# A fused attention and mixture-of-experts layer on one Trainium2 core: the softmax division goes from VectorE to ScalarE, over four buffers, with a pair's two transposes in one step

## What is computed

```
scores = einsum('bhqd,bhkd->bhqk', qh, kh) * DH ** (-0.5)
window_mask = (j <= i) & (j >= i - W)          # W = 64
scores = where(window_mask, scores, -1e+30)
probs = softmax(scores, axis=-1)
out = einsum('bhqk,bhkd->bhqd', probs, vh)
...
x = x + tanh(g_xattn) * (out @ wo.T)
x = x + tanh(g_ffn) * moe(layernorm(x))
```

## Time and profile before

| what | value |
|---|---|
| median of 3 runs | 578.61 us (577.44 to 578.98) |
| the profiled execution | 576.19 us |
| its span, first to last instruction | 574.4 us |
| mean granted TensorE clock | 0.982 |
| attention, some 30 to 352 us: busy TensorE / VectorE / ScalarE / GpSimd | 284.4 / 273.1 / 188.2 / 187.2 us of 322 |

### The profile page before, as it was taken

The page is one execution under the profiler, slowest core; times in us unless marked ns, Lnnn a source line. Parts: engine busy times, 40 slices in busy tenths (PEclk is TensorE's granted clock), DMA queues, the critical chain, the costliest instruction groups (busy, mean ns, idle before and its releaser), DMA issues.

```text
span 574.4 us, 13053 instructions
## 1 busy us (share of the span) xinstructions
PE 526.0 (92%) x4914; PEld 458.3 (80%) x4914; DVE 416.1 (72%) x1139; ACT 292.8 (51%) x832; POOL 220.9 (38%) x123
## 2 busy tenths in 40 slices
PE   8968889999699999699897989989999999999997
PEld 5557677888597888588777878978998898899996
DVE  5987879779979879988968895655465646564444
ACT  3275556565375556366635775544445443533332
POOL 2897846447447545635834841620010001000000
PEclk9999989999999999899989989989999999999999
DMA  6621311111022011011201045600800090036000
GB/s 237 195 69 57 107 48 61 34 34 33 2 71 70 2 34 33 2 34 34 70 2 34 20 125 185 222 1 3 294 36 1 11 322 1 1 91 242 1 1 37
DMA packets 20173, 41.02 MB, mean 71 GB/s; under 512 B 2896, under 2 KB 3152, under 8 KB 20112
## 3 DMA queue, kind: packets, MB, share of 16 engines
q1 hardware_dynamic: 20112, 40.20, 22.4%
HBM read 30.62 MB, written 2.23 MB: 57 GB/s over the span
## 4 chain that ended last, share of the span: by engine, by line
PE 56%; DVE 24%; issue 11%; ACT 3%; POOL 3%; DMA 1%; SPq 0%; DVEq 0%; ACTq 0%; POOLq 0%
PE ring L761 37%; PE psS L761 8%; DVE arena L594 5%; DVE sneg L713 5%; DVE prob L725 4%; PE psO L959 3%; PE psS L928 3%; PE psT L940 3%; DVE xn L574 2%; DVE arena L591 2%; DVE wl L661 1%; DMA x<-in_x 1%; POOL wl L396 1%; POOL arena L415 1%; PE psT L901 1%
## 5 line engine op out<-in xcount | busy, mean ns | idle before, releaser
L498 ACT ACTIVATE prob<-sneg,nmax 128x128 f32<-128x128 f32 x256 | 99.8, 395 | 71.9 <-DVE nmax L713 70.7
L761 PE MATMUL ring<-xTh,wh 128*128 128x512 f32 x272 | 111.1, 408 | 4.9 <-POOL wl L396 2.3
L411 POOL TENSOR_TENSOR arena<-arena,sin 128x1024 f32<-128x1024 f32 (+1 forms) x34 | 78.0, 2295 | 93.0 <-DVE arena L591 93.0
L761 PE MATMUL ring<-xTl,wh 128*128 128x512 f32 x272 | 106.9, 393 | 0.0
L761 PE MATMUL ring<-xTh,wl 128*128 128x512 f32 x272 | 106.2, 390 | 0.0
L442 ACT ACTIVATE sneg<-ring 128x512 f32<-128x512 f32 x72 | 43.3, 601 | 109.5 <-PE ring L761 103.6
L640 DVE TENSOR_TENSOR prob<-sneg,arena 128x512 f32<-128x512 f32 x64 | 44.2, 690 | 69.1 <-ACT sneg L442 69.1
L415 POOL TENSOR_TENSOR arena<-arena 128x1024 f32<-128x1024 f32 (+1 forms) x34 | 85.4, 2513 | 2.7
L761 PE MATMUL ring<-wh,oTh 128*128 128x256 f32 x272 | 77.7, 286 | 1.4 <-DVE oTl L648 0.9
L725 DVE TENSOR_TENSOR prob<-prob,rinv 128x512 f32<-128x512 f32 x64 | 76.2, 1190 | 2.2
L761 PE MATMUL ring<-wl,oTh 128*128 128x256 f32 x272 | 76.0, 279 | 0.0
(11 more groups left out here) (111 smaller groups left out, 1123.9 us busy)
## 6 DMA issues: line engine op xcount, KB each, us to landing
arena<-gate_scratch SPq DMA_DIRECT2D x64, 256.0 KB, 6.3
raw<-in_e SPq DMA_DIRECT2D x18, 256.0 KB, 2.8
raw<-in_w SPq DMA_DIRECT2D x16, 256.0 KB, 2.9
arena<-arena SPq DMA_DIRECT2D x16, 256.0 KB, 3.1
arena<-arena SPq DMA_DIRECT2D x16, 192.0 KB, 3.4
craw<-in_ctx SPq DMA_DIRECT2D x4, 512.0 KB, 3.5
x<-in_x SPq DMA_DIRECT2D x4, 512.0 KB, 4.6
out<-x SPq DMA_DIRECT2D x8, 256.0 KB, 2.7
```

The source lines that it names most:

```text
L411: link(pool.tensor_tensor(part, part, sin[:, :].unsqueeze(1).to_broadcast(part.shape), ALU.mult))
L498: last = act.activation(prob[:, c % 3, t, :], sneg[:, c % 2, t, :], ACT.Exp, bias=nmax[:, c % 4, t:t + 1], scale=-1.0, accum_out=rsum[:, c ...
L761: last = pe.matmul(out, a, b, start=start and i == 0 and j == 0, stop=stop and i == n - 1 and j == 2, skip_group_check=check)
```

## The change

1. The multiplication of the probabilities goes from one VectorE instruction of 128x512 per head (L725) to four ScalarE instructions of 128x128, which are Copy with `rinv` as a scale per row. They stand in ScalarE's queue after the exponentials of the next head. VectorE keeps the reciprocal (`invert`).
2. `sneg`, `prob` and `rinv` have four buffers each. Two of `sneg` lie in `arena`.
3. VectorE does `score_max` for both heads of a pair in the even step.
4. The transposes of the pair `2p`, `2p+1` stand in step `2p + 3`: the first ahead of the jobs, the second after them, and likewise their copies out on ScalarE.
5. GpSimd's rotation of q stands at k = 1, that of k has its multiplication at k = 2 and its addition at k = 3.

The core of the diff:

```diff
-        prob = sb("prob", [P, 3, TT, P])
+        prob = sb("prob", [P, BUFS, TT, P])
...
+        transposed = {2 * p + 3: 2 * p for p in range(CHUNKS // 2)}
...
+            for c, jobs in steps:
+                u, k = divmod(c, G)
+                if u + 1 < UNITS:
+                    if k == 1:
+                        turn(0, u + 1)
+                        join(0, u + 1)
+                    if k == 2 and u:
+                        turn(1, u + 1)
+                    if k == 3 and u:
+                        join(1, u + 1)
+                for job in jobs:
+                    do(job)
...
+            def divide(c):
+                act.wait_ge(s_inv, c + 1)
+                for t in range(TT):
+                    last = act.activation(prob[:, c % BUFS, t, :], prob[:, c % BUFS, t, :], ACT.Copy,
+                                          scale=rinv[:, c % BUFS, t:t + 1])
+                last.then_inc(s_norm, 1)
...
             for c, jobs in steps:
-                if 2 <= c <= CHUNKS + 1:
-                    copy_transposed(c - 2)
+                if c in transposed:
+                    copy_transposed(transposed[c])
                 if c in attended:
                     round_att(attended[c])
                 if c < CHUNKS:
                     softmax_numerator(c)
+                if 1 <= c <= CHUNKS:
+                    divide(c - 1)
                 for job in jobs:
                     do(job)
+                if c in transposed:
+                    copy_transposed(transposed[c] + 1)
...
-                if c >= 2:
-                    dve.wait_ge(s_exp, c - 1)
+                if c >= BUFS:
+                    dve.wait_ge(s_exp, c - BUFS + 1)
...
-                dve.wait_ge(s_inv, c + 1)
-                dve.tensor_tensor(prob[:, c % 3, :, :], prob[:, c % 3, :, :],
-                                  rinv[:, c % 2, :].unsqueeze(2).to_broadcast([P, TT, P]),
-                                  ALU.mult).then_inc(s_norm, 1)
...
             for c, jobs in steps:
-                if c < CHUNKS:
+                if c < CHUNKS and c % 2 == 0:
                     score_max(c)
+                    score_max(c + 1)
                 if 1 <= c <= CHUNKS:
-                    divide(c - 1)
+                    invert(c - 1)
...
-                if 2 <= c <= CHUNKS + 1:
-                    transpose_probs(c - 2)
+                if c in transposed:
+                    transpose_probs(transposed[c])
                 for job in jobs:
                     do(job)
+                if c in transposed:
+                    transpose_probs(transposed[c] + 1)
```

More of the change, by code:

```diff
@@ L83, in build @@
         rw_parts = sb("rw_parts", [P, KC, 2, NR], F32R)
-        sizes = dict(swap=(2, 2, L), qT=(2, 2, L), kT=(2, 2, W + L), spare=(1, 2, 896),
+        sizes = dict(swap=(2, 2, L), qT=(2, 2, L), kT=(2, 2, W + L), idle=(1, 1, L), late=(2, TT, P), spare=(1, 1, 256),
                      v_al=(2, TT, GD), v_sh=(2, TT, GD))
@@ L91, in build @@
             at += a * b * c
-        idle = cuts["spare"][:, 0, 0, 0:L]
+        idle = cuts["idle"][:, 0, 0, :]
         swap = cuts["swap"]
@@ L96, in build @@
         gate_bc = arena[:, 0:NR * L].rearrange("p (e n) -> p e n", e=NR)
-        sneg = sb("sneg", [P, 2, TT, P])
-        prob = sb("prob", [P, 3, TT, P])
+        sneg_a = sb("sneg", [P, 2, TT, P])
+        sneg = [sneg_a[:, 0, :, :], sneg_a[:, 1, :, :], cuts["late"][:, 0, :, :], cuts["late"][:, 1, :, :]]
+        prob = sb("prob", [P, BUFS, TT, P])
         pT = sb("pT", [P, 4, TT, P])
@@ L390, in _, with turn, join @@
             pool.wait_ge(pool_init, 1)
+            def turn(i, n):
+                for done, pairs in rotations(n):
+                    part = swap[:, i, pairs, :]
+                    pool.wait_ge(qk_swap[i], done)
+                    link(pool.tensor_tensor(part, part,
+                                            sin[:, :].unsqueeze(1).to_broadcast(part.shape),
+                                            ALU.mult))
+            def join(i, n):
+                dst = (qT[:, n % 2, :, :], kT[:, n % 2, :, W:])[i]
+                for done, pairs in rotations(n):
+                    pool.wait_ge(qk_mul[i], done)
+                    pool.tensor_tensor(dst[:, pairs, :], dst[:, pairs, :], swap[:, i, pairs, :],
+                                       ALU.add).then_inc(qk_rot[i], 1)
             def do(job):
@@ L402, in do @@
                                        ALU.subtract).then_inc(c_lo, 1)
-                elif kind in "qk":
+                elif kind in "qk" and n < 1 + (kind == "k"):
                     i = "qk".index(kind)
-                    dst = qT[:, n % 2, :, :] if kind == "q" else kT[:, n % 2, :, W:]
                     if n == 0:
@@ L421, in do @@
                                        ALU.pow).then_inc(ln_rstd, 1)
-            for job in jobs_a + [j for n in range(NS, N + 2) for j in after[n]]:
+            for job in prologue:
                 do(job)
+            for c, jobs in steps:
[10 more added lines that the diff above has]
+                    do(job)
+            for n in range(NS, N + 2):
+                for job in after[n]:
+                    do(job)
         @block.scalar
@@ L494, in softmax_numerator @@
                 act.wait_ge(s_max, c + 1)
-                if c >= 3:
-                    act.wait_ge(p_pe, c - 2)
+                if c >= BUFS:
+                    act.wait_ge(p_pe, c - BUFS + 1)
                 for t in range(TT):
-                    last = act.activation(prob[:, c % 3, t, :], sneg[:, c % 2, t, :], ACT.Exp,
+                    last = act.activation(prob[:, c % BUFS, t, :], sneg[c % BUFS][:, t, :], ACT.Exp,
                                           bias=nmax[:, c % 4, t:t + 1], scale=-1.0,
@@ L709, in score_max @@
                     dve.wait_ge(in_const, consts)
-                if c >= 2:
-                    dve.wait_ge(s_exp, c - 1)
+                if c >= BUFS:
+                    dve.wait_ge(s_exp, c - BUFS + 1)
                 for t in range(TT):
-                    last = dve.tensor_tensor_reduce(sneg[:, c % 2, t, :], psS[c % 2][:, t, :],
+                    last = dve.tensor_tensor_reduce(sneg[c % BUFS][:, t, :], psS[c % 2][:, t, :],
                                                     mask[:, min(t, 1), :], -SCALE, -MASKED * 1e3,
@@ L939, in transpose_probs @@
                 for t in range(TT):
-                    last = pe.transpose(psT[:, t, :], prob[:, c % 3, t, :], ident[:, :])
+                    last = pe.transpose(psT[:, t, :], prob[:, c % BUFS, t, :], ident[:, :])
                 last.then_inc(p_pe, 1)
```

15 lines of the change are left out of this document (9 added, 6 removed).

## The result

The changed kernel takes **583.56 us** (median of 5, 581.28 to 585.40), the kernel before 577.58 (median of 5, 576.48 to 578.98): a ratio of **1.0099, with the 95% interval 1.0067 to 1.0131**. It is 6 us slower. The forecast was 589.0 with the range 572 to 604, and slower the likeliest sign.

A forecast was written before the change was run, and what follows sets the result against it. TensorE was taken as the bound, 31 us of its attention waits ending with VectorE. -2.1 (normal units) + 3.3 (norm units) + 6.4 (start) + 3.2 (end) = +10.8 on the profiled 576.2, so 587.0, median 589 us; range 572 to 604.

The forecast's parts named there:

- The bound, and the loop on ScalarE: Attention: TensorE bounds; its VectorE waits go, but `values` waits 0.8 us for the second head's copy behind ScalarE's division.
- rival 2: Attention: ScalarE, idle 42%, has room; half of the 31 us of waits go, none come; 563 us, chance 0.10.
- The copy's price: ScalarE's division: 0.30 us per 128x128 instruction, 1.2 us a head, 77 us in all.
- Rivals 1 and 4: ScalarE's division: cheap copies at 0.19 us, 575 us, chance 0.14; dear copies at 0.39 us, 607 us, chance 0.12.
- rival 1: ScalarE's division: cheap copies at 0.19 us an instruction, 0.44 us shorter a head; -14.5 us, 575 us, chance 0.14.
- Normal units: Seven units without a layer norm: 18.45 us each for 18.73, -0.3 us each, -2.1 in all.
- Norm units: Units 2, 6, 10 with the layer norm: `values` waits 4.8 us for 4.76; +1.1 us each, +3.3.
- Start: Units 0 and 1: weight copies on ScalarE and GpSimd's late addition, with clock losses, cost +6.4 us.
- +4.6 at the product of unit 1: Start, unit 1: the product at 63.28 us begins at about 67.9 without the clock, which adds +1.8.
- Rival 3: Start and norm units: GpSimd and the norm cost nothing new, both fall to old times; 580 us, chance 0.12.
- End: Units 12 to 16: -3.2, +1.0, +4 for units 14 and 15, +1.4 behind the table load; sum +3.2 us.
- The chances: Whole kernel: slower 0.65, within 0.3% 0.08, faster 0.27; forecast of 583 to 597 us 0.52.

The follow-up runs named there:

- E1: Changed kernel, but ScalarE divides an odd step's head after the pair's second transposed copy, not ahead of it: 568.99 us, ratio 0.9832.
- E9: E8 with the layer norm placed earlier as in E5: 551.26 us, ratio 0.9534 to the kernel before.
- E2: Changed kernel with a constant scale in place of each row's reciprocal, so probabilities are not divided by their sums: 574.97 us, ratio 0.9947.
- E6: Changed kernel with four idle matmuls filling each of the three 4.33 us waits in the norm units: 577.06 us, ratio 0.9981.
- E8: E1 with GpSimd's rotations at their old places, as in E4: 563.42 us, ratio 0.9738.
- E4: Changed kernel with GpSimd's rotations at their old places, q at k = 0 and k at k = 1: 581.52 us, ratio 1.0063.
- E7: E3 with the low part of the attention output ahead of reciprocal and division in VectorE's queue: 567.77 us, ratio 0.9829.
- E3: Changed kernel with the division back on VectorE, directly behind the reciprocal, the rest of the change kept: 590.04 us, ratio 1.0216.
- E12: Kernel before the change with only the layer norm moved earlier, as in E5: 568.96 us, ratio 0.9845.
- E11: E7 (division on VectorE) with GpSimd's old places from E4 and the norm's earlier place from E5: 556.8 us, ratio 0.9618.
- E5: Changed kernel with the next batch's layer-norm statistics two steps earlier and its norm one step earlier: 568.52 us, ratio 0.9839.

## Why the prediction was right

**The bound, and the loop on ScalarE: right, and shown.** The waits on VectorE went and waits of `values` on the second head's copy came. E1 keeps all work and moves it behind that copy: 14.6 us less. ScalarE's share did not decide it, as E9 with the same work shows; rival 2, which argued from that share, falls.

**The copy's price: right.** 0.295 us start to start for the 0.30 taken; the half with q and k showed no wait, as forecast. The Trainium skill, "ScalarE: Activation LUTs", section "What ACT_TABLE_LOAD costs", charges 93 ns for a per-row operand; E2 took it away and the mean fell by 94 ns, so trace and page agree. (Without that charge the page's figures give 0.20, and not the 0.19 that the prediction names.) Rivals 1 and 4, cheap and dear copies, fall with this number. Without the operand the instructions start 0.20 us apart (E2), and the kernel takes 574.97 us, where rival 1 had 0.19 and 575. That the two times meet is in part chance: rival 1 took 14.5 us off the forecast, and E2 took 8.6 off the measured time, 11.7 by the traces.

**Normal units: right in kind, the term mis-sized.** The wait in the half with v and y was 0.45 us where 0.8 had been worked out, and the unit 18.10 for 18.45. The second copy ended 8.2 us behind the end of `values` (151.95 - 143.75), where the sum had 8.45. Besides, the first unit behind each norm unit took 19.2 us before (86.45 to 105.66) and not 18.73, and fell to 18.1 too; the prediction had counted it like the others. Six units gave 4.8 us and not 1.8.

**Norm units: the mechanism right, the size not.** The wait was 4.33 for 4.8, released by the chain that was named. All three were equal; the prediction had the longest in units 6 and 10. The wait in the second half was 0.9 for 1.2. But the units cost 5.6 us more than before and not 3.3. Two terms were mis-sized. In the kernel before such a unit took 24.84 to 25.17 us, and not 25.4. And the prediction took one clock loss of 1.7 us from the earlier trace rows and left it as it was, as if it were fixed for a wait of the same length. The clock was at 1.2 GHz for 6.7, 3.4 and 6.8 us around the new waits, against 3.3 to 3.5 before, and E6 prices this at 2.6, 1.3 and 2.5 us; unit 2 lost 1.5 us more to the low clock that it had from the start. The work without the clock was over-counted, 24.8 us for the 24.1 of E6, and that hid part of it.

**Start: nearly right.** +7.8 for +6.4. The first part is +5.2 at the first pair (45.43, against 45.1 forecast). GpSimd's part is real, as E8 shows, but most of the +7.8 is not GpSimd's: with its old order the start is 2.3 us shorter (E4), and with ScalarE's copy ahead of the division 4.1 (E1, 64.97 us to c = 8). Of the +4.6 at the product of unit 1 the prediction shows the working of 2.2 and 1.7 only. It added two clock losses, 3.5 us in all. The trace has 1.2 GHz from 39.2 to 49.4 and from 66.4 to 73.4 us, where the kernel before had none ahead of 73.7; what this cost the start no run separates. The scores of unit 2 waited 3.31 us and not 4; the profile names no releaser, but with GpSimd's old order (E4, E8) this wait is gone:

```profile
67.19 1.98 PE L970 MATMUL psS<-arena 64*64 64x128 f32 x32 [3.31 <-issue]
```

Rival 3 falls: GpSimd and the norm do cost something new.

**End: right by its parts in two of three.** The two last halves took 19.5 us, from 335.02 to 354.51, against 14.9 before: +4.6 for +4. The last copy behind the table load cost +1.3 for +1.4, as these rows of the changed kernel show:

```profile
357.98 1.28 ACT L476 ACT_TABLE_LOAD   x1
359.27 0.60 ACT L476 ACTIVATE sneg<-ring 128x512 f32<-128x512 f32 x1
359.76 0.59 ACT L548 ACTIVATE pT<-psT 128x512 f32<-128x512 f32 x1
360.41 1.33 PE L1001 MATMUL psO<-pT,arena 128*64 128x64 f32 x20 [1.68 <-ACT pT L548]
```

Units 11 to 14 gained 4.7 us (81.39 to 76.70) where 2.5 had been forecast. So the sum was +1.2, and +2.9 had been expected with unit 11.

**The total.** Forecast +10.8 on the profiled execution, measured +9.2; 1.4 us (start) and 2.3 (norm units) were missing, and 3.0 (normal units), 1.7 (end) and 0.7 (experts) were too much. That the total came so near is luck in part: errors of 3.7 and 5.4 us stood against each other. The medians differ by 6.0 and not by 9.2, since the profiled runs lie at the long end of one spread and below the other; hence 583.6 and not 589. The chances leaned to slower, and rightly.

## What to carry to other kernels

Do not ask how busy the engine is that gets the work, but what will stand behind it in that engine's queue, and follow every consumer there: by order alone E1 and E9 win 15 and 32 us on the changed kernel, and E7 wins 22 on E3. An instruction on which the bounding engine waits goes ahead of one that has slack, and a long shared job, like the layer norm here, goes where nobody waits behind it. Price the parts of a change apart: here the buffers, the pairings and one order together were worth 12 us (E12 against E11), and the engine of the division 5.5 (E11 against E9). Look at the granted clock behind each long wait, because the wait's own length in the profile is only a part of its price.

## What the runs showed of the hardware

**The clock's price varies behind equal waits.** Three waits of 4.33 us each came with 6.7, 3.4 and 6.8 us at 1.2 GHz, and the halves behind them took 13.61, 12.34 and 13.46 us; with 3.7 us of products in the wait TensorE kept its full 2.4 GHz, and all three took 11.00. Why the low stretch was twice as long in two of them stays open.

**VectorE beside GpSimd waits for whole instructions.** In E7 two equal divisions stand 3 us apart, one started beside GpSimd's addition and one after it:

```profile
120.33 2.40 POOL L408 TENSOR_TENSOR arena<-arena 128x1024 f32<-128x1024 f32 x1
...
120.38 2.90 DVE L761 TENSOR_TENSOR prob<-prob,rinv 128x512 f32<-128x512 f32 x1
...
123.40 0.69 DVE L761 TENSOR_TENSOR prob<-prob,rinv 128x512 f32<-128x512 f32 x1
```

The first ends 0.55 us behind the addition, about its own free length of 0.69. So it is throughout E7: the 34 of its 64 divisions that began with GpSimd idle took 0.69 us each, and of the 30 that began beside a GpSimd instruction 29 ended 0.53 to 0.56 us behind it. The Trainium skill, "SBUF — State Buffer", section "SBUF: two separate sides", says that for a VectorE instruction with two inputs in SBUF, against a GpSimd instruction that reads SBUF, the port pair shared by these two engines is a lock that the one that starts first holds for the whole instruction, while the other is blocked; the division is such an instruction, and these rows agree. The layer norm took 4.67 us across two GpSimd instructions and 1.37 with GpSimd idle (E5). ScalarE's division showed nothing of this: its instructions took 386 to 402 ns in the changed kernel between 140 and 152 us, where GpSimd was busy until 149.2.
